# Quantized-weight stage of a vision tower: ScalarE converts one half of the codes ahead, one more mask slot on each side, and buffers placed elsewhere

## The chip, the core and the metric

The kernel runs on one NeuronCore of a Trainium2 chip. Times are microseconds of device time, the median of several executions. The engines are PE (TensorE), DVE (VectorE), ACT (ScalarE), POOL (GpSimd) and SP (SyncE, which here only issues DMA transfers). Each works through its own instructions in order and waits on semaphores.

## What is computed

The input is 32 sequences of 64 positions with 64 complex coefficients each; a filter with 64 modes spreads it to 1024 features, and two layers follow. Cut to its steps, the reference is:

```
h = _L0_tok_ref(L0_tok_A_abslog, L0_tok_A_phase, x, 1024)      # sum over 64 modes of exp(dtA * t)
h = h + _L0_attn_ref(_layernorm(h, axis=-1), Wq, Wk, Wv, Wo)   # 16 heads, rotary, causal
h = h + _L0_ffn_ref(_layernorm(h, axis=-1), w_idx, absmax, bias)
h = h + _L1_attn_ref(_layernorm(h, axis=-1), ...)              # selective state space scan
h = h + _L1_ffn_ref(_layernorm(h, axis=-1), ...)               # base + top-2 of 8 low-rank experts
```

The part that matters here is the first step and the weights of the third:

```
# the filter: K[h, l] = sum_n Cc[h, n] * exp(dtA[h, n] * l), h = 2 * K.real
# the weights: 1024 x 1024 codes of 0 to 15
w = NF4_CODE[w_idx.reshape(-1, BLOCK)] * absmax[:, None]
return jnp.einsum('bsi,oi->bso', x, w) + bias
```

## The kernel before

Everything is float32 in SBUF. The 2048 tokens are worked on in four blocks of 512 (`NBLK`), and most of the kernel is, per block, a row of weight strips of 128 x 1024 that ACT and POOL split in two parts each and PE multiplies. That begins behind an **opening stage**, the only part in which the change moves instructions. It does two things side by side.

*Weights.* The codes are turned into weights in 16 **halves** (`HALVES`; half i is one half of strip i // 2). For a half, SP loads the codes into `dqi` (two slots, i % 2), ACT converts them to bf16 in `dqf` (two slots; L573). The 16 codes stand in 8 pairs. For 5 pairs DVE writes a mask by comparing with the code (`mkd`, L1272), for 3 pairs ACT does with Abs and Relu (`away`, then `mka`, L579 and L583). PE multiplies each mask with diagonals of the code's value and adds up in `psx` (L853): per half 30 matmuls on DVE's masks, then 14 on ACT's. DVE then multiplies by the block maxima (`weights`, L1283, run behind the masks of the next half) and SP stores the result. Mask slots are rings: `RING_ACT` = 2 and `RING_DVE` = 3; a mask waits until PE has used the one that was in its slot (`s_useda`, `s_usedd`).

*The filter.* DVE and ACT build tables of Sin and Exp (DVE L1288 to L1374, ACT L594 to L606); DVE makes the factors `high` and `low` of eight positions (`powers(g)`, L1388 to L1395), PE multiplies them (`filters(g)`, L875, 32 matmuls), and ACT copies the result to the filtered sequence `hT` (`copies(g)`, L589). There are 8 groups g.

*The order* is written out by hand. Halves 0 to 4 (`EARLY`) stand ahead of the groups. Behind the filters of group g stand the halves of `LATE[g]`, on PE, DVE and ACT alike:

```
LATE = [[5, 6], [7], [8, 9], [10], [11, 12], [13], [14], [15]]
```

On ACT the copies of group g stand behind the masks of these halves, and `filters(g + 1)` needs room in `psg` that the copies make. SP's loop over the halves decides when codes are loaded:

```
for i in range(HALVES):
    m, q = i // 2, i % 2
    if i + 2 < HALVES:
        sp.wait_ge(s_dqf, i + 1)
        load_codes(i + 2)
    sp.wait_ge(s_dq, i + 1)
    sp.dma_start(w_ffn[m, :, q * HALF:(q + 1) * HALF], dqw[:, q, :]).then_inc(s_dqw[q], 16)
```

`s_dq` counts the halves whose weights DVE has written, `s_dqf` the converted ones. Behind the last half SP stores three blocks of `hT` to memory (L454), and DVE waits for two of these stores (`v.wait_ge(s_keep, 32)`) before it writes the first `xc` (L1415).

Buffers are placed by hand: each `with ExitStack()` block starts again at the address where the block before it started, so what is in different blocks lies over one another. `hT` lies over `u` and the 16 slots of [P, T] behind it.

Of the kernel before, what the change touches and what calls it, by code (L numbers as in the profile page):

```python
# [14 lines left out]
F32 = mybir.dt.float32  # L15
F32R = mybir.dt.float32r
# [6 lines left out]
P = 128  # L23
NSEQ, S, E = 32, 64, 1024
NMODE = 64
KC = E // P
NB = 8
NBLK = NSEQ // NB
T = NB * S
# [18 lines left out]
NQ = NST // 4  # L48
XT = T // P
# [82 lines left out]
PAIRS = 8  # L132
BY_ACT = 3
BY_DVE = PAIRS - BY_ACT
RING_ACT, RING_DVE = 2, 3
HALF = KC * P // 2
HALVES = 2 * KC
FG = 8
# [37 lines left out]
def tower(nc, ins, out, nblk=NBLK, stop=9):  # L176
    with ExitStack() as ctx:
# [3 lines left out]
        def sb(name, shape, dt=F32, c=ctx):  # L181
            return c.enter_context(nc.sbuf_tensor("sb_" + name, shape, dt))
# [14 lines left out]
        def C(name, a=0, n=None):  # L197
            c0, w = CCOL[name]
            return cst[:, c0 + a:c0 + (w if n is None else a + n)]
# [35 lines left out]
        u = sb("u", [P, DC, T])  # L235

        with ExitStack() as c:
            xc = sb("xc", [P, KC, T], F32, c)
            xh = sb("xh", [P, KC, T], F32R, c)
            xl = sb("xl", [P, KC, T], F32R, c)  # L240
            ah = sb("ah", [P, KC, T], F32R, c)
            al = sb("al", [P, KC, T], F32R, c)
            rstd = sb("rstd", [P, T], F32, c)
            rcos = sb("rcos", [P, NB, S], F32, c)
            rsin = sb("rsin", [P, NB, S], F32, c)
            with ExitStack() as c2:
                qc = sb("qc", [P, T], F32, c2)
                qs = sb("qs", [P, T], F32, c2)
                kc = sb("kc", [P, T], F32, c2)
                ks = sb("ks", [P, T], F32, c2)  # L250
                vf = sb("vf", [P, T], F32, c2)
                vT = sb("vT", [P, T], F32, c2)
                sm = sb("sm", [P, NB, S], F32, c2)
                pT = sb("pT", [P, T], F32, c2)
                ao = sb("ao", [P, NB, S], F32, c2)
                smx = sb("smx", [P, 2, NB], F32, c2)
            with ExitStack() as c2:
                sq = sb("sq", [P, 2, T], F32, c2)
                tA = sb("tA", [P, T], F32, c2)
                tB = sb("tB", [P, T], F32, c2)  # L260
                cv = sb("cv", [P, 2, NB, S], F32, c2)
                rt = sb("rt", [P, 8, 32], F32, c2)
        with ExitStack() as c:
            sb("over_x", [P, 3 * KC, T], F32, c)
            wT = sb("wT", [P, T], F32, c)
            w16 = sb("w16", [P, T // P, P], F32, c)
            hwh = sb("hwh", [P, T], F32R, c)
            hwl = sb("hwl", [P, T], F32R, c)
        with ExitStack() as c:
            sb("over_ah", [P, 4 * KC, T], F32, c)  # L270
            gt = sb("gt", [P, 2, T], F32, c)
            xsh = sb("xsh", [P, T], F32R, c)
            xsl = sb("xsl", [P, T], F32R, c)
            pick = sb("pick", [P, NST, P], F32R, c)
        with ExitStack() as c:
            cb_hi = sb("cb_hi", [P, 2, NB, 4, S], F32, c)
            wst = sb("wst", [P, RING, NB, 4, S], F32, c)
            twin = sb("twin", [P, 2, T], F32, c)
            gin = sb("gin", [P, 2, T], F32, c)
            dgB = sb("dgB", [P, XT, NQ, 2, 4, 32], F32, c)  # L280
            dA = sb("dA", [P, RING, NB, 4, S], F32, c)
            duT = sb("duT", [P, 2, T], F32, c)
            du = sb("du", [P, T], F32, c)
            spt = sb("spt", [P, 2, T], F32, c)
            dlt = sb("dlt", [P, 2, T], F32, c)
            wdt = sb("wdt", [RDT, 2, P], F32, c)
            dgD = sb("dgD", [P, 2, P], F32, c)
        with ExitStack() as c:
            yh = sb("yh", [P, DC, T], F32R, c)
            yl = sb("yl", [P, DC, T], F32R, c)  # L290
            lb = [sb(f"lb{n}", [P, KC, P], F32R, c) for n in range(2)]
        psg = ctx.enter_context(nc.psum_tensor("psg", [P, 4, 512], F32))
        psx = ctx.enter_context(nc.psum_tensor("psx", [P, 4, 512], F32))

# [267 lines left out]
        def _(act):  # L562
# [1 line left out]
            act.sem_inc(s_strip, CR_STRIP)  # L564
            act.wait_ge(s_mode, 80)

            def masks(i):

                q = i % 2
                act.wait_ge(s_dqi[q], i // 2 * 32 + 32)  # L570
                if i >= 2:
                    act.wait_ge(s_mkd, (i - 1) * BY_DVE)
                A(dqf[:, q, :, :], dqi[:, q, :, :], ACT.Copy).then_inc(s_dqf, 1)  # L573
                act.wait_ge(s_dqf, i + 1)
                for j in range(BY_ACT):
                    at = i * BY_ACT + j
                    if at >= 2:
                        act.wait_ge(s_mka, at - 1)
                    A(away[:, at % 2, :, :], dqf[:, q, :, :], ACT.Abs, bias=C("minus", BY_DVE + j, 1)).then_inc(s_away, 1)  # L579
                    act.wait_ge(s_away, at + 1)  # L580
                    if at >= RING_ACT:
                        act.wait_ge(s_useda, at - RING_ACT + 1)
                    A(mka[:, at % RING_ACT, :, :], away[:, at % 2, :, :], ACT.Relu, bias=C("one"), scale=-1.0).then_inc(s_mka, 1)  # L583

            def copies(g):

                for n in range(4 * g, 4 * g + 4):
                    act.wait_ge(s_filt, n + 1)
                    A(hT[:, :, :, :, 2 * n:2 * n + 2].rearrange("p b k c e -> p (b k c) e"),  # L589
                      psg[:, n % 4, :].rearrange("p (e x) -> p x e", e=2), ACT.Copy).then_inc(s_hT, 1)  # L590

            masks(0)
            act.wait_ge(s_tab, TAB_SIN[0])
            A(tab[:, 0, :, :], tab[:, 0, :, :], ACT.Sin, bias=0.0).then_inc(s_tabA, 1)  # L594
            masks(1)
            act.wait_ge(s_tab, TAB_SIN[1])
            A(tab[:, 1, :, :], tab[:, 1, :, :], ACT.Sin, bias=0.0).then_inc(s_tabA, 1)
            masks(2)
            act.wait_ge(s_tab, TAB_SIN[2])
            A(tabs[:, :, :, :], tabs[:, :, :, :], ACT.Sin, bias=0.0).then_inc(s_tabA, 1)  # L600
# [1184 lines left out]
```

## Time and profile before

| | us |
|---|---|
| median of 3 runs (4456.22 to 4457.9) | 4457.05 |
| profiled execution, its own time | 4457.86 |
| its span | 4455.4 |
| PE busy | 4153.1 (93% of the span) |
| DVE busy | 2748.4 (62%) |
| ACT busy | 2013.5 (45%) |
| POOL busy | 2180.9 (49%) |

The span runs from the first to the last instruction on the engines. A share over the whole span says little about the opening stage, which is the first 250 us of it and has limits of its own. `PEclk` is the granted clock of PE as a share of full speed: 1.00 is 2.4 GHz, 0.50 is 1.2 GHz.

### The profile page before, as it was taken

How to read it: one execution, taken by the hardware profiler on the slowest of the kernel's cores; microseconds unless marked ns; L12 is line 12 of the kernel's file. 1: busy time of each engine (PE TensorE's matmuls, PEld its weight loads, DVE VectorE, ACT ScalarE, POOL GpSimd, SP SyncE). 2: the span in 40 equal slices, each digit the busy share in tenths (PEclk: the TensorE clock that was granted, in tenths of full speed). 3: DMA queues.
4: the chain of work that ended last, by engine and by line, in shares of the span. 5: the costliest groups of instructions: out<-in, count | busy, mean ns of one | idle time of the engine just before them, and what ended most of it. 6: DMA issues, size and time to landing. Idle time of an engine off the chain costs nothing.

```text
span 4455.4 us, 58954 instructions
## 1 busy us (share of the span) xinstructions
PE 4153.1 (93%) x22688; PEld 2736.2 (61%) x22688; DVE 2748.4 (62%) x2907; ACT 2013.5 (45%) x2938; POOL 2180.9 (49%) x912
## 2 busy tenths in 40 slices
PE   3879999899999999999999999999999999989998
PEld 1557777444677777544577777644377777744467
DVE  7744463899344374599634455399934447379943
ACT  5632244777232233677422224477632223467731
POOL 0023333788523333588633333388833333378852
PEclk7989999999989999999989999999999999999998
DMA  3332223000322223200122223300022222310021
GB/s 93 84 120 72 71 100 109 29 14 16 113 71 72 76 66 121 68 14 17 62 86 84 71 76 109 100 12 17 34 95 83 74 67 81 125 42 17 14 83 62
DMA packets 93813, 303.18 MB, mean 68 GB/s; under 512 B 11648, under 2 KB 15872, under 8 KB 91008
## 3 DMA queue, kind: packets, MB, share of 16 engines
q1 hardware_dynamic: 84352, 282.98, 19.5%
q10 hardware_dynamic: 9216, 16.78, 1.0%
q8 instruction: 172, 2.82, 0.3%
q14 instruction: 73, 0.60, 0.0%
HBM read 255.68 MB, written 44.04 MB: 67 GB/s over the span
## 4 chain that ended last, share of the span: by engine, by line
PE 81%; DVE 10%; issue 6%; ACT 1%; DMA 1%; POOL 0%; DVEq 0%; POOLq 0%; ACTq 0%
PE psg L896 39%; PE psx L1074 9%; PE psg L1089 8%; DVE sb_wst L1610 6%; PE psg L923 5%; PE psx L911 3%; PE psg L932 2%; PE psx L1005 2%; PE psg L1103 1%; PE psx L1018 1%; PE psg L1051 1%; PE psx L1116 1%; PE psg L1100 1%; PE psx L1204 1%; DVE psg L1583 1%
## 5 line engine op out<-in xcount | busy, mean ns | idle before, releaser
L521 POOL TENSOR_TENSOR sb_wl<-sb_raw,sb_wh 128x1024 fp32r<-128x1024 f32 x388 | 973.6, 2512 | 2064.5 <-ACT sb_wh L619 2064.2
L1610 DVE TENSOR_TENSOR_SCAN sb_wst<-sb_dA,psx 128x1024 f32<-128x1024 f32 x512 | 1140.1, 2271 | 36.8 <-ACT sb_dA L742 23.7
L619 ACT ACTIVATE sb_wh<-sb_raw 128x1024 fp32r<-128x1024 f32 x388 | 408.3, 1053 | 624.4 <-PE psg L896 323.3
L1074 PEld LDWEIGHTS psx<-sb_dgB,sb_duT 64*128 64x128 f32 x4096 | 358.7, 189 | 526.6 <-DVE sb_wst L1610 266.4
L742 ACT ACTIVATE sb_dA<-sb_dlt,sb_a_sb 128x504 f32<-128x504 f32 x1024 | 646.4, 705 | 61.2 <-DVE sb_wst L1610 55.5
L1074 PE MATMUL psx<-sb_dgB,sb_duT 64*128 64x256 f32 x4096 | 590.8, 408 | 85.6 <-DVE sb_wst L1610 83.8
L554 POOL TENSOR_TENSOR sb_wst<-sb_wst,sb_cb_lo 128x1024 f32<-128x1024 f32 x256 | 599.2, 2362 | 90.1 <-DVE sb_wst L1610 90.1
L554 POOL TENSOR_TENSOR sb_wst<-sb_wst,sb_cb_hi 128x1024 f32<-128x1024 f32 x256 | 598.4, 2358 | 75.5 <-DVE sb_wst L1610 75.5
L1089 PE MATMUL psg<-sb_wst,sb_cst 64*64 64x512 f32 x4096 | 564.8, 624 | 10.3 <-POOL sb_wst L554 9.6
L896 PE MATMUL psg<-sb_xh,sb_wh 128*128 128x512 f32 x2112 | 558.4, 407 | 0.0
L896 PE MATMUL psg<-sb_xh,sb_wl 128*128 128x512 f32 x2112 | 522.4, 389 | 0.0
L896 PE MATMUL psg<-sb_xl,sb_wh 128*128 128x512 f32 x2112 | 521.9, 389 | 0.0
L896 PEld LDWEIGHTS psg<-sb_xh,sb_wh 128*128 128x128 f32 x2112 | 398.7, 192 | 106.3 <-issue 24.6
L896 PEld LDWEIGHTS psg<-sb_xh,sb_wl 128*128 128x128 f32 x2112 | 396.6, 188 | 84.3
L896 PEld LDWEIGHTS psg<-sb_xl,sb_wh 128*128 128x128 f32 x2112 | 396.4, 188 | 82.3
L1089 PEld LDWEIGHTS psg<-sb_wst,sb_cst 64*64 64x64 f32 x4096 | 109.2, 133 | 212.2 <-issue 212.2
L1648 DVE TENSOR_TENSOR psg<-psg,sb_rstd 128x512 f32<-128x512 f32 x64 | 44.8, 700 | 306.3 <-PE psg L896 306.3
L1680 DVE TENSOR_TENSOR sb_h<-sb_h,psg 128x512 f32 x32 | 22.0, 688 | 258.1 <-PE psg L896 137.2
L1572 DVE SCALAR_TENSOR_TENSOR sb_cv<-psg,sb_conv,sb_cv 128x504 f32<-128x504 f32 (+2 forms) x192 | 141.0, 735 | 27.8 <-DVE sb_cv L1570 4.2
L923 PE MATMUL psg<-sb_xh,sb_wh 128*128 128x512 f32 x192 | 119.4, 622 | 29.5 <-ACT sb_xh L627 29.5
L911 PE MATMUL psx<-sb_sq,sb_cst 128*128 128x512 f32 x256 | 143.1, 642 | 0.0
L733 ACT ACTIVATE sb_twin<-psg 128x512 f32<-128x512 f32 x128 | 69.5, 595 | 161.9 <-PE psg L1089 161.9
(269 smaller groups left out, 5233.6 us busy)
## 6 DMA issues: line engine op xcount, KB each, us to landing
sb_raw<-in_w SPq DMA_DIRECT2D x360, 512.0 KB, 3.5
sb_raw<-w_ffn_dequantized SPq DMA_DIRECT2D x32, 512.0 KB, 3.2
gates<-sb_gt ACTq DMA_DIRECT2D x64, 256.0 KB, 2.2
sb_gin<-gates SPq DMA_DIRECT2D x64, 256.0 KB, 2.6
sb_dqi<-in_w_idx SPq DMA_DIRECT2D x32, 256.0 KB, 4.9
h_after_tok<-sb_h SPq DMA_DIRECT2D x4, 2048.0 KB, 8.7
sb_h<-h_after_tok SPq DMA_DIRECT2D x4, 2048.0 KB, 7.8
out<-sb_h SPq DMA_DIRECT2D x4, 2048.0 KB, 7.3
```

What stands on the lines that cost most here:

```text
L521: pool.tensor_tensor(rest(b, i0), raw[:, i0 % RAW, :, :], high(b, i0).bitcast(F32), ALU.subtract).then_inc(s_wl, 1)
L554: pool.tensor_tensor(x, x, cb, ALU.mult).then_inc(s_p, 1)
L619: A(high(b, i0), raw[:, i0 % RAW, :, :], ACT.Copy).then_inc(s_wh, 1)
L742: ins_ = A(dA[:, (m * NQ + k) % RING, :, n, 1:S], dlt[:, m % 2, :].rearrange("p (b s) -> p b s", b=NB)[:, :, 1:S], ACT.Exp, scale=a_sb[:, ...
L896: ins_ = mm(psg[:, bank, :], w_[:, s_, k, :], x_[:, k0 + k, :], start=start and n == 0, stop=stop_ and n == 3 * KC - 1)
L911: mm(psx[:, 1, :], C("mean"), sq[:, k % 2, :], start=(k == 0), stop=(k == KC - 1)).then_inc(s_squ, 1)
L923: mm(psg[:, banks[s], :], w_[:, slot(b, i0 + s), k, :], X[:, kk, :], start=(k == 0 and n == 0 and not (one_chunk and s)), stop=False)
L932: ins_ = mm(psg[:, banks[s], :], wh[:, slot(b, i0 + s), k, :], Xl[:, kk, :], start=False, stop=(k == KC - 1 and not (one_chunk and not s)))
L1074: ins_ = mm(psx[:, 2 * j + r, :].rearrange("p (a t e) -> p a t e", a=8, e=2)[:, :, :, e], duT[r0:r0 + 64, m % 2, i * P:(i + 1) * P], dgB[r ...
L1089: ins_ = mm(psg[64 * c:64 * c + 64, r, :], C("fold")[r0:r0 + 64, :], wst[r0:r0 + 64, (m * NQ + k) % RING, :, 2 * half + c, :], start=(k == ...
L1572: ins_ = stt(y[:, :, d:S], x[:, :, 0:S - d], tap(3 - d), y[:, :, d:S], ALU.mult, ALU.add)
L1610: v.tensor_tensor_scan(wst[:, x, 4 * j:4 * j + 4, :, :].rearrange("p b n s -> p (b n s)"), dA[:, x, 4 * j:4 * j + 4, :, :].rearrange("p b ...
```

## The change

`RING_ACT` becomes 3 and `RING_DVE` 4. On ACT the conversion leaves `masks(i)` and becomes a function `converted(i)`; `masks(0)` calls it for halves 0 and 1, each later `masks(i)` calls `converted(i + 1)` ahead of its own masks. Its waits stay the same expressions of the half that it converts. To make room for the slots, buffers of the opening stage behind `mka` lie 2 to 4 KB higher per partition, and of the buffers that are used later `ah` and `al` now lie over the last two blocks of `hT`, `xc`, `xh` and `xl` behind them; `lb0`, `lb1`, `dgB`, `wst`, `twin`, `gin`, `gt`, `yh`, `yl` and others move with them. Every buffer that moves does so by a multiple of 2 KB.

```diff
-RING_ACT, RING_DVE = 2, 3
+RING_ACT, RING_DVE = 3, 4
...
+            ah = sb("ah", [P, KC, T], F32R, c)
+            al = sb("al", [P, KC, T], F32R, c)
             xc = sb("xc", [P, KC, T], F32, c)
             xh = sb("xh", [P, KC, T], F32R, c)
             xl = sb("xl", [P, KC, T], F32R, c)
-            ah = sb("ah", [P, KC, T], F32R, c)
-            al = sb("al", [P, KC, T], F32R, c)
...
         with ExitStack() as c:
-            sb("over_x", [P, 3 * KC, T], F32, c)
+            lb = [sb(f"lb{n}", [P, KC, P], F32R, c) for n in range(2)]
...
         with ExitStack() as c:
-            sb("over_ah", [P, 4 * KC, T], F32, c)
+            sb("over_a", [P, 2 * KC, T], F32, c)
...
             cb_hi = sb("cb_hi", [P, 2, NB, 4, S], F32, c)
+            dgB = sb("dgB", [P, XT, NQ, 2, 4, 32], F32, c)
...
-            dgB = sb("dgB", [P, XT, NQ, 2, 4, 32], F32, c)
...
         with ExitStack() as c:
+            sb("over_ah", [P, KC, T], F32, c)
             yh = sb("yh", [P, DC, T], F32R, c)
             yl = sb("yl", [P, DC, T], F32R, c)
-            lb = [sb(f"lb{n}", [P, KC, P], F32R, c) for n in range(2)]
...
-            def masks(i):
+            def converted(i):
 
                 q = i % 2
                 act.wait_ge(s_dqi[q], i // 2 * 32 + 32)
                 if i >= 2:
                     act.wait_ge(s_mkd, (i - 1) * BY_DVE)
                 A(dqf[:, q, :, :], dqi[:, q, :, :], ACT.Copy).then_inc(s_dqf, 1)
+
+            def masks(i):
+
+                q = i % 2
+                if i == 0:
+                    converted(0)
+                if i + 1 < HALVES:
+                    converted(i + 1)
                 act.wait_ge(s_dqf, i + 1)
```

On PE, DVE, POOL and SP the order of instructions is the same before and after. On ACT it moves as follows. First the start of the program, before, up to the first Sin (L594) and the conversion of half 1; the brackets name the semaphores that an instruction waits on:

```order
L573 ACTIVATE sb_dqf<-sb_dqi 128x1024 [waits s_mode]
L579 ACTIVATE sb_away<-sb_dqf,sb_cst 128x1024 [waits s_dqf]
L583 ACTIVATE sb_mka<-sb_away,sb_cst 128x1024 [waits s_away]
L579 ACTIVATE sb_away<-sb_dqf,sb_cst 128x1024
L583 ACTIVATE sb_mka<-sb_away,sb_cst 128x1024 [waits s_away]
L579 ACTIVATE sb_away<-sb_dqf,sb_cst 128x1024 [waits s_mka]
L583 ACTIVATE sb_mka<-sb_away,sb_cst 128x1024 [waits s_useda,s_away]
L594 ACT_TABLE_LOAD
L594 ACTIVATE sb_tab<-sb_tab 128x2048 [waits s_tab]
L573 ACTIVATE sb_dqf<-sb_dqi 128x1024 [waits s_dqi1]
```

and now (behind L573 the lines are 8 higher):

```order
L573 ACTIVATE sb_dqf<-sb_dqi 128x1024 [waits s_mode]
L573 ACTIVATE sb_dqf<-sb_dqi 128x1024 [waits s_dqi1]
L587 ACTIVATE sb_away<-sb_dqf,sb_cst 128x1024 [waits s_dqf]
L591 ACTIVATE sb_mka<-sb_away,sb_cst 128x1024 [waits s_away]
L587 ACTIVATE sb_away<-sb_dqf,sb_cst 128x1024
L591 ACTIVATE sb_mka<-sb_away,sb_cst 128x1024 [waits s_away]
L587 ACTIVATE sb_away<-sb_dqf,sb_cst 128x1024 [waits s_mka]
L591 ACTIVATE sb_mka<-sb_away,sb_cst 128x1024 [waits s_away]
L602 ACT_TABLE_LOAD
L602 ACTIVATE sb_tab<-sb_tab 128x2048 [waits s_tab]
L573 ACTIVATE sb_dqf<-sb_dqi 128x1024 [waits s_mkd,s_dqi0]
```

The third mask of half 0 no longer waits on `s_useda`. The conversion behind the Sin is that of half 2 instead of half 1, and it now waits on `s_mkd` too.

The second place is group 0 of the filter: half 5 and the head of half 6 on ACT. Before:

```order
L573 ACTIVATE sb_dqf<-sb_dqi 128x1024 [waits s_mkd,s_dqi1]
L579 ACTIVATE sb_away<-sb_dqf,sb_cst 128x1024 [waits s_mka,s_dqf]
L583 ACTIVATE sb_mka<-sb_away,sb_cst 128x1024 [waits s_useda,s_away]
...
L583 ACTIVATE sb_mka<-sb_away,sb_cst 128x1024 [waits s_useda,s_away]
L573 ACTIVATE sb_dqf<-sb_dqi 128x1024 [waits s_mkd,s_dqi0]
L579 ACTIVATE sb_away<-sb_dqf,sb_cst 128x1024 [waits s_mka,s_dqf]
```

and now:

```order
L573 ACTIVATE sb_dqf<-sb_dqi 128x1024 [waits s_mkd,s_dqi0]
L587 ACTIVATE sb_away<-sb_dqf,sb_cst 128x1024 [waits s_mka,s_dqf]
L591 ACTIVATE sb_mka<-sb_away,sb_cst 128x1024 [waits s_useda,s_away]
...
L591 ACTIVATE sb_mka<-sb_away,sb_cst 128x1024 [waits s_useda,s_away]
L573 ACTIVATE sb_dqf<-sb_dqi 128x1024 [waits s_mkd,s_dqi1]
L587 ACTIVATE sb_away<-sb_dqf,sb_cst 128x1024 [waits s_mka,s_dqf]
```

The rows are alike but for the slot of `dqi`: ahead of half 5's masks stands the conversion of half 6 (slot 0) instead of half 5 (slot 1), ahead of half 6's masks that of half 7.

## Rows read from the trace of the kernel before

A row of a timeline has the start and the duration in us, the engine (PEq, SPq: its queue), the line, the operation, out<-in, the number of instructions merged and, in brackets, how long the engine idled before them and what ended that. A row of windows has the stretch, its length, then busy time and number of instructions of PE, PE's weight loads, DVE, ACT and POOL, then the granted clock, the DMA share and GB/s. "DMA to landing" is the time from the start of a request to its arrival.

**Rows 1.** The page: its first line

```profile
span 4455.4 us, 58954 instructions
```

**Rows 2.** Windows of the opening stage

```profile
7.00:120.00 113.00, 39.38 (x226) 19.88 (x227) 92.77 (x132) 56.59 (x51) 0.00 (x0) 0.74 0.34 85
120.00:250.00 130.00, 114.22 (x737) 75.73 (x736) 87.54 (x140) 94.32 (x104) 0.00 (x0) 0.99 0.31 81
```

**Rows 3.** Waits from 0 to 250 us: total, times, longest

```profile
ACT sb_mka L583 <- PE psx L853: 87.2, 13, 26.2
```

**Rows 4.** Timeline of DVE, half 0

```profile
22.52 0.49 DVE L1272 TENSOR_SCALAR sb_mkd<-sb_dqf,sb_cst 128x1024 bf16<-128x1024 bf16 x1 [0.89 <-PE psx L853]
23.80 0.49 DVE L1272 TENSOR_SCALAR sb_mkd<-sb_dqf,sb_cst 128x1024 bf16<-128x1024 bf16 x1 [0.79 <-PE psx L853]
```

**Rows 5.** Timeline of DVE and ACT, up to the Exp

```profile
39.03 0.69 DVE L1283 TENSOR_TENSOR sb_dqw<-psx,sb_dqa 128x512 f32<-128x512 f32 x1
...
58.28 0.96 DVE L1328 TENSOR_TENSOR sb_etabs<-sb_mode,sb_cst 128x768 f32<-128x768 f32 x1
...
66.21 1.15 ACT L583 ACTIVATE sb_mka<-sb_away,sb_cst 128x1024 bf16<-128x1024 bf16 x1 [14.47 <-PE psx L853]
...
70.25 1.91 ACT L604 ACTIVATE sb_etab<-sb_etab 128x2048 f32<-128x2048 f32 x1
...
72.92 2.29 DVE L1335 TENSOR_TENSOR sb_tab<-sb_tab,sb_etab 128x2048 f32<-128x2048 f32 x1 [9.12 <-ACT sb_etabs L605]
```

**Rows 6.** Timeline of DVE, SP, PE and ACT, 117 to 175 us

```profile
117.36 9.59 PE L875 MATMUL psg<-sb_high,sb_low 128*128 128x256 f32 x32 [18.64 <-DVE sb_low L1395]
...
127.77 0.49 DVE L1272 TENSOR_SCALAR sb_mkd<-sb_dqf,sb_cst 128x1024 bf16<-128x1024 bf16 x1 [0.80 <-PE psx L853]
128.42 0.49 DVE L1272 TENSOR_SCALAR sb_mkd<-sb_dqf,sb_cst 128x1024 bf16<-128x1024 bf16 x1 [0.16 <-PE psx L853]
128.82 0.68 DVE L1283 TENSOR_TENSOR sb_dqw<-psx,sb_dqa 128x512 f32<-128x512 f32 x1
...
130.40 1.26 SPq L399 DMA_DIRECT2D sb_dqi<-in_w_idx  x2
...
140.60 7.14 PE L875 MATMUL psg<-sb_high,sb_low 128*128 128x256 f32 x32 [0.17 <-ACT sb_hT L589]
...
153.05 0.41 PE L853 MATMUL psx<-sb_mka,sb_dg 128*64 128x512 bf16 x2 [0.66 <-ACT sb_mka L583]
153.64 1.53 PE L875 MATMUL psg<-sb_high,sb_low 128*128 128x256 f32 x6 [0.18 <-ACT sb_hT L589]
...
165.95 1.04 ACT L573 ACTIVATE sb_dqf<-sb_dqi 128x1024 bf16<-128x1024 int32 x1
...
173.70 1.58 ACT L589 ACTIVATE sb_hT<-psg 128x512 f32<-128x512 f32 x3
...
174.44 0.89 PE L875 MATMUL psg<-sb_high,sb_low 128*128 128x256 f32 x3 [0.18 <-ACT sb_hT L589]
```

**Rows 7.** Requests into sb_dqi: landing of all requests, then at 131.0 and 185.7

```profile
DMA to landing us min/median/max: 4.0/4.9/15.7
...
DMA to landing us min/median/max: 4.8/5.1/5.4
...
DMA to landing us min/median/max: 5.2/5.7/6.1
```

**Rows 8.** Windows: PE's busy time and granted clock

```profile
117.40:122.20 4.80, 4.80 (x11) 3.83 (x12) 4.80 (x9) 0.00 (x0) 0.00 (x0) 0.50 0.00 0
245.00:248.50 3.50, 1.57 (x14) 0.48 (x10) 0.69 (x1) 2.88 (x5) 0.00 (x0) 1.00 0.18 69
248.90:251.90 3.00, 3.00 (x4) 1.45 (x5) 0.00 (x0) 1.12 (x1) 0.00 (x0) 0.50 0.52 132
```

**Rows 9.** Timeline of DVE, end of the stage

```profile
247.27 0.69 DVE L1283 TENSOR_TENSOR sb_dqw<-psx,sb_dqa 128x512 f32<-128x512 f32 x1 [3.21 <-PE psx L853]
266.20 1.88 DVE L1415 TENSOR_TENSOR sb_xc<-sb_hT,psx 128x512 f32<-128x512 f32 x3 [18.24 <-DMA h_after_tok<-sb_hT]
```

## The prediction

> **What bounds the kernel now.** The profiled execution took 4457.86 us, of which 4455.4 us are the span [rows 1]; 2.5 us lie around it. The median of the three timed runs is 4457.05 us. I sum shifts inside the span, and carry them over to the median one for one.
>
> Every instruction that the change moves, and every ring that it widens, is in the opening stage, from 0 to about 250 us: the order of SP, POOL, PE and DVE is the same in both programs. So I read that stage alone. The windows split it in two [rows 2]. Up to 120 us DVE is busy for 92.8 of 113 us and PE for 39: DVE's chain of small table operations sets the pace. From 120 to 250 us PE is busy for 114 of 130 us, ACT for 94, DVE for 88: there PE and ACT hand work to each other. The waits of the stage then say what the three wait for [rows 3]: ACT's mask writes waited 87.2 us in 13 places for PE to release a mask slot. DVE's mask writes wait for PE too [rows 4, 6]. Only what lies on the path counts of either.
>
> **First part: DVE's chain up to 120 us.** With three slots DVE can write masks 0 to 2 of a half, then waits for PE to use mask 0 before it writes mask 3, and for mask 1 before mask 4. In half 0 these two waits end at 22.52 and 23.80 [rows 4]. With four slots mask 3 needs no wait, and mask 4 takes the place that mask 3 had: it starts at 22.52. DVE is done 1.28 us sooner. PE runs at its slow clock at the start of each of the first five halves, so this repeats: 5 x 1.28 = 6.4 us.
>
> The second gain is one long wait. ACT's third mask of half 2 stood 14.47 us behind PE (slot 0 of two was still in use), the Sin of the tables and the Exp stood behind it, and DVE's product with the Exp waited 9.12 us more, until 72.92 [rows 5]. With three slots the third mask of a half needs only a slot that was used in the half before, so ACT can reach the Exp before its input exists. What is late next? ACT must now convert half 3 ahead of the masks of half 2, and SP requests the codes of half 3 only after DVE has written the weights of half 0. These ended at 39.7 [rows 5], now 2 x 1.28 us sooner, at 37.2; with a trip of 6.9 us (below) the codes are there at 44.1. The conversion and six mask operations take 7.8 us (165.95 to 173.70 in [rows 6]), Sin and table load 2.9 us (from the end of L583 at 67.4 to 70.25 in [rows 5]): ACT is ready for the Exp at 54.8. Its input comes from DVE at 59.2 - 2.6 = 56.7 [rows 5], so ACT has 1.9 us of cover. The Exps take 2.7 us (70.25 to 72.92) and end at 59.4; DVE, 3 x 1.28 us ahead of before, wants them at 72.92 - 9.12 - 3.84 = 60.0. So the whole 9.1 us goes. Together, half 5's dequantization on PE starts 6.4 + 9.1 = **15.5 us earlier**, at 111.4.
>
> **Second part: the wait that takes its place.** `masks(i)` now begins with `converted(i + 1)`. Behind that instruction, on an engine that works in order, stand the six operations of half i's masks and the four copies of the filtered sequence; PE's last three pairs of half i and the next group of filters wait for those. The conversion needs the codes of half i + 1. SP requests them only after it has stored the weights of half i - 2, which DVE writes behind its masks of half i - 1. (The conversion also waits for those masks themselves, `s_mkd`; that wait ends just ahead of the weights, so it is never the later one.) Where two halves stand behind one group of filters (groups 0, 2 and 4), this trip becomes the longest path:
> - In half 5 DVE's last two masks start at 127.77 and 128.42 [rows 6]; with one slot more the last starts at 127.77, which saves 0.65 us. The weights then end 2.6 - 0.65 = 1.95 us after PE began the half (129.50 before; PE began at 126.9, when its cold filters of 9.59 us ended).
> - From the end of the weights to the codes: SP starts its second request of 256 KB at about 131.0, 1.5 us later [rows 6], and it lands 5.4 us after that [rows 7]: 6.9 us. Another landed 6.1 us after its start, the quickest of all 4.0 us [rows 7], so the trip is 5.5 to 7.6 us. I take 6.9 for group 0, 6.7 for the others.
> - From the start of a conversion to the start of the next filters, with no wait between: 165.95 to 174.44 [rows 6], 8.5 us.
>
> Group 0, from PE's start of half 5 to the next filters: 1.95 + 6.9 + 8.5 = 17.35 us; before, 126.9 to 140.60, 13.7 us. **3.6 us longer.** Groups 2 and 4, from filters to filters: 7.1 (the filters, [rows 6]) + 1.95 + 6.7 + 8.5 = 24.25 us; before, 153.64 to 174.44, 20.8 us. **3.45 us longer, twice.**
>
> Groups 1, 3, 5, 6 and 7 have one half each, and there the codes landed long before. What is left is PE's own work. Before, PE waited 0.66 us for ACT's last mask, its last pair took 0.41, and the filters came 0.18 us later still [rows 6]; the filters at 153.64 would have started near 152.6 without it. **5 x 1.05 = 5.2 us shorter.** Half 15's conversion waits for the weights of half 12, one group earlier; in group 6 that lands some 4 us into the filters and costs 0.5 us: 3.9 + 8.5 = 12.4 us against 11.9.
>
> **Third part: PE's clock.** In the new two-half groups PE starts the second half 12.1 us behind the group's filters and has used DVE's masks at 15.4. ACT starts its conversion at 15.75 and has the first mask 3.4 us later: PE idles 3.8 us, and then 1.6 us ahead of each of the next two masks, which come 2.2 us apart and take 0.64 and 0.2 us: some 1.5 us of work in 9. The trace shows what such a stretch does. From 245.0 to 248.5 PE was busy for 1.57 of 3.5 us, and the 3 us behind it ran at a granted clock of 0.50, that is 1.2 GHz instead of 2.4 [rows 8]. PE will be emptier than that in these stretches, so I expect the filters behind each of the three groups to start at 1.2 GHz. What that costs, one group shows: the filters at 117.36 started at 0.50 [rows 8] and took 9.59 us, those at 140.60 took 7.14 [rows 6]. **3 x 2.4 = 7.2 us.** The Trainium skill (TensorE: Matmul & The Clock Gate, HAM oscillation) says the same of bursts with DMA waits between: the wait lets the array be throttled again, and the next burst starts cold, every time. By that rule the sum is the one below with the 7.2 us; if the clock stayed up, it would be 7.2 us lower. This kernel's own rows side with the rule.
>
> **Fourth part: the end of the stage and the places.** SP stores the last weights behind PE's last pair (DVE's operation at 247.27), then the filtered sequence; DVE waits 18.24 us for those stores until 266.20 [rows 9]. `v.wait_ge(s_keep, 32)` still stands there, though `xc` no longer lies over the filtered sequence, so this wait stays whole and the stage after shifts as a block. The other buffers keep their sizes and their instructions; no row of before shows a duration that depends on a buffer's place, so I put that at 0, within 2 us either way.
>
> **Sum.** -15.5 + 3.6 + 2 x 3.45 - 5.2 + 0.5 = -9.7; with the clock, -9.7 + 7.2 = **-2.5 us**. That gives 4455.4 us for the profiled execution, and 4454.6 us for the median.
>
> **Rivals.**
> - *The clock stays up.* Then -9.7: 4447.4 us. For it: from 120 to 250 us the granted clock was 0.99 in the mean, waits and all [rows 2]. Against it: the fall in [rows 8] came with more work than these gaps hold.
> - *Slower: DVE's wait for the Exp comes back.* If the codes of half 3 land later than the 1.9 us of cover allows, DVE waits again. From about 4.4 us late on, the kernel is slower than before; if the whole 9.1 us return, -2.5 + 9.1 = +6.6: 4463.7 us. Longer trips push the same way: 0.7 us more at each of the three groups (7.4 to 7.6 us, the upper end of [rows 7]) is +2 us. For it: one load of codes took 15.7 us, against a median of 4.9 [rows 7]; it was requested near the start, among the loads of the whole input. It is half 2's, and lands near 30, in time for half 1's masks to end near 38. Against it: the codes of half 3 are requested at 38 us, when those loads are done.
> - *The trip is hidden.* If something else holds the second conversion off the path, the pairs would run at ACT's pace. Two halves are then 2 x 7.8 us and four copies 2 us, 17.6 us against 20.8, which saves 3.2 us in each of the three groups. With no fall of the clock that is -15.5 - 9.6 - 5.2 = -30 us: 4427 us. Nothing in the order of SP speaks for it, since the request stands behind the weights.
>
> **How the numbers follow.** A measurement of this kernel tells about 0.2% (8.9 us) from no change, so the bounds are 4448.1 and 4466. Forecast (three slow starts, long trips), 4450 to 4459: 0.62. Clock stays up, at least in part, 4443 to 4450: 0.20. Exp wait or longer trips, 4459 to 4466: 0.11. Trip hidden, below 4440: 0.05. Anything slower still: 0.02. The range takes in the first two and half of the third: 4444 to 4461. Faster by over 0.2%: most of the second and all of the fourth, 0.2. Slower by over 0.2%: 0.04. The same: 0.76.
>
> **What would show it** (lines numbered as before; behind L573 the changed file is 8 lines longer). Right: DVE L1335's wait is gone and the L875 filters start near 102 us; ACT's L573 waits for the DMA of `sb_dqi` at three to five places with 3 us or more each; ACT no longer waits at its last mask; the second, fourth and sixth group of filters (about 129, 167 and 206 us) take some 9.5 us with a granted clock near 0.5 at their start; DVE's last L1283 starts near 245 us; from there on each instruction has the distance that it had. Wrong: filters of 7.1 us behind the pairs (then the clock term goes), pairs of 21 us or less (the trip is off the path), or a stage after 250 us that is longer or shorter by itself (places matter).

## The result and the profile after

| | before | after |
|---|---|---|
| median, us | 4457.45 (20 runs, 4455.94 to 4459.47) | 4450.41 (20 runs, 4445.77 to 4452.36) |
| profiled execution, us | 4457.86 | 4449.22 |
| its span, us | 4455.4 | 4447.1 |

The ratio of after to before is 0.9983, with a 95% interval of 0.9976 to 0.999: 7.0 us less. The time lies inside the predicted range, 4.2 us below the predicted 4454.6. The gain itself, 7.0 us, is nearly three times the 2.5 us that were forecast. It is within 0.2% of before, though the interval leaves out 1. The head of the page after, beside [rows 1]:

```profile
span 4447.1 us, 58953 instructions
## 1 busy us (share of the span) xinstructions
PE 4153.7 (93%) x22688; PEld 2736.7 (62%) x22688; DVE 2746.8 (62%) x2907; ACT 2013.7 (45%) x2938; POOL 2180.6 (49%) x912
```

No engine has other work; only waits changed. The windows of the opening stage, beside [rows 2]:

```profile
7.00:120.00 113.00, 52.20 (x326) 28.73 (x326) 105.32 (x154) 59.06 (x54) 0.00 (x0) 0.79 0.39 97
120.00:250.00 130.00, 111.40 (x650) 70.81 (x650) 73.59 (x118) 92.72 (x103) 1.04 (x1) 0.92 0.29 82
```

Up to 120 us DVE is busy for 105.3 us where it was 92.8: it waits 12.5 us less in this stretch. From 120 to 250 us the mean granted clock fell from 0.99 to 0.92. The waits from 0 to 250 us, beside [rows 3]:

```profile
ACT sb_dqf L573 <- DMA sb_dqi<-in_w_idx: 74.7, 12, 26.1
...
DVE sb_mkd L1280 <- PE psx L861: 48.9, 19, 9.5
...
PE psx L861 <- ACT sb_mka L591: 20.1, 13, 3.7
...
ACT sb_etab L612 <- DVE sb_etabs L1336: 1.7, 1, 1.7
```

ACT's 87.2 us of waits for PE at its mask write are gone. In their place stand 74.7 us at the conversion, for codes. Some of that is harmless, like the wait for PE before it; what counts is whether PE then waits for ACT. The timeline of DVE and ACT in the first part, beside [rows 4] and [rows 5]:

```profile
22.40 0.49 DVE L1280 TENSOR_SCALAR sb_mkd<-sb_dqf,sb_cst 128x1024 bf16<-128x1024 bf16 x1 [0.49 <-PE psx L861]
...
59.77 2.28 DVE L1343 TENSOR_TENSOR sb_tab<-sb_tab,sb_etab 128x2048 f32<-128x2048 f32 x1
...
43.81 1.06 ACT L573 ACTIVATE sb_dqf<-sb_dqi 128x1024 bf16<-128x1024 int32 x1 [2.51 <-DMA sb_dqi<-in_w_idx]
...
56.61 1.91 ACT L612 ACTIVATE sb_etab<-sb_etab 128x2048 f32<-128x2048 f32 x1 [1.71 <-DVE sb_etabs L1336]
```

In the first five halves DVE now has at most one wait per half instead of two, and its product with the Exp (L1343) starts at 59.77 without a wait. ACT had the codes of half 3 at 43.81 and still waited 1.71 us for the Exp's input. The timeline of PE, DVE, SP and ACT over the first groups, beside [rows 6]:

```profile
111.22 3.43 PE L861 MATMUL psx<-sb_mkd,sb_dg 128*64 128x512 bf16 x30
...
112.50 0.68 DVE L1291 TENSOR_TENSOR sb_dqw<-psx,sb_dqa 128x512 f32<-128x512 f32 x1
...
114.08 1.26 SPq L399 DMA_DIRECT2D sb_dqi<-in_w_idx  x2
...
119.74 1.06 ACT L573 ACTIVATE sb_dqf<-sb_dqi 128x1024 bf16<-128x1024 int32 x1 [26.07 <-DMA sb_dqi<-in_w_idx]
...
115.99 3.40 PE L861 MATMUL psx<-sb_mkd,sb_dg 128*64 128x512 bf16 x30
123.07 0.84 PE L861 MATMUL psx<-sb_mka,sb_dg 128*64 128x512 bf16 x6 [3.67 <-ACT sb_mka L591]
125.29 1.49 PE L861 MATMUL psx<-sb_mka,sb_dg 128*64 128x512 bf16 x6 [1.38 <-ACT sb_mka L591]
127.51 0.64 PE L861 MATMUL psx<-sb_mka,sb_dg 128*64 128x512 bf16 x2 [0.73 <-ACT sb_mka L591]
128.11 8.56 PE L883 MATMUL psg<-sb_high,sb_low 128*128 128x256 f32 x32
...
141.47 7.17 PE L883 MATMUL psg<-sb_high,sb_low 128*128 128x256 f32 x32
...
165.13 8.83 PE L883 MATMUL psg<-sb_high,sb_low 128*128 128x256 f32 x32
...
178.75 7.17 PE L883 MATMUL psg<-sb_high,sb_low 128*128 128x256 f32 x32
```

This is the whole mechanism in one place. DVE writes weights (of half 4) at 112.50; SP requests codes (of half 7) behind them at 114.08; ACT gets them at 119.74; PE, which had finished DVE's masks of half 6 at 119.4 (115.99 + 3.40), waits 3.67, 1.38 and 0.73 us for ACT's masks; and the filters behind the pair take 8.56 us instead of 7.17. The windows show the clock there, beside [rows 8]:

```profile
119.60:123.00 3.40, 0.00 (x0) 0.00 (x0) 3.40 (x7) 3.23 (x4) 0.00 (x0) 1.00 0.81 195
124.40:127.90 3.50, 1.88 (x8) 0.49 (x8) 3.47 (x6) 3.47 (x5) 0.00 (x0) 0.50 0.01 2
128.20:130.90 2.70, 2.70 (x7) 2.17 (x8) 0.00 (x0) 2.70 (x5) 0.00 (x0) 0.50 0.02 6
131.20:136.40 5.20, 5.20 (x26) 4.48 (x24) 0.00 (x0) 5.10 (x6) 0.00 (x0) 1.00 0.00 0
```

The granted clock was at 2.4 GHz while PE idled, fell to 1.2 GHz behind the idle stretch, and was back at 2.4 GHz some 3 us into the filters. The end of the stage on DVE and SP, beside [rows 9]:

```profile
240.95 0.69 DVE L1291 TENSOR_TENSOR sb_dqw<-psx,sb_dqa 128x512 f32<-128x512 f32 x1 [3.02 <-PE psx L861]
260.01 1.88 DVE L1423 TENSOR_TENSOR sb_xc<-sb_hT,psx 128x512 f32<-128x512 f32 x3 [18.37 <-DMA h_after_tok<-sb_hT]
...
243.78 0.81 SPq L446 DMA_DIRECT2D sb_raw<-in_w  x2
```

The last weights come 6.3 us sooner (247.27 before), and DVE's wait for the stores stays: 18.37 us against 18.24.

### The profile page after: what moved, and what is told of

The parts are those of the page before. It is cut to its first block, busy times and chain, and to the rows that moved or that the text cites. A ratio compares the mean times of both kernels' runs of the same rounds, so it can differ in the third digit from the quotient of the medians.

```text
span 4447.1 us, 58953 instructions
## 1 busy us (share of the span) xinstructions
PE 4153.7 (93%) x22688; PEld 2736.7 (62%) x22688; DVE 2746.8 (62%) x2907; ACT 2013.7 (45%) x2938; POOL 2180.6 (49%) x912
## 4 chain that ended last, share of the span: by engine, by line
PE 81%; DVE 10%; issue 6%; ACT 1%; DMA 1%; POOL 0%; DVEq 0%; POOLq 0%; ACTq 0%
PE psg L904 39%; PE psx L1082 9%; PE psg L1097 8%; DVE sb_wst L1618 6%; PE psg L931 5%; PE psx L919 3%; PE psg L940 2%; PE psx L1013 2%; PE psg L1111 1%; PE psx L1026 1%; PE psg L1059 1%; PE psx L1124 1%; PE psg L1108 1%; PE psx L1212 1%; DVE psg L1591 1%
## 5 line engine op out<-in xcount | busy, mean ns | idle before, releaser
L1618 DVE TENSOR_TENSOR_SCAN sb_wst<-sb_dA,psx 128x1024 f32<-128x1024 f32 x512 | 1140.4, 2271 | 37.3 <-ACT sb_dA L750 23.7
```

Source lines behind the costliest of these rows:

```text
L1618: v.tensor_tensor_scan(wst[:, x, 4 * j:4 * j + 4, :, :].rearrange("p b n s -> p (b n s)"), dA[:, x, 4 * j:4 * j + 4, :, :].rearrange("p b ...
```

## The experiments

The theory is the prediction's: the longer rings take waits off the path, and converting ahead puts a trip of the codes and a cold PE on it. The rival readings are that the conversion ahead is what removes the waits, that the moved buffers matter, and that the trip is a matter of DMA speed and not of where the request stands. Each kernel starts from after; "old order" is this edit:

```diff
             def masks(i):
-                if i == 0:
-                    converted(0)
-                if i + 1 < HALVES:
-                    converted(i + 1)
+                converted(i)
```

**The long rings alone** (old order, `RING_ACT, RING_DVE = 3, 4`).

> The longer rings and the new places stay, the conversion goes back: half i is converted at the head of its own masks. If my account holds, the gain of 15.5 us ahead of half 5 stays, the trip for the codes leaves the path, and the groups of two halves run at ACT's pace: about 17.4 us from filters to filters instead of 23.7 to 24.1, group 0 about 10.2 instead of 16.9, and the filters behind them start at full clock. Sum -15.5 - 3.5 - 6.8 - 5.2 = -31: about 4426 us, 24 us faster than the changed kernel. Rival: the conversion ahead is itself worth something, since DVE no longer waits for it (16.7 us of such waits before); then this kernel is slower than the changed one, above 4450 us.

Measured: 4425.87 us, ratio 0.993 (0.9914 to 0.9945) to before: 32 us less than before and 24.5 less than after. Timeline of PE and DVE:

```profile
101.04 10.02 PE L880 MATMUL psg<-sb_high,sb_low 128*128 128x256 f32 x32 [18.40 <-DVE sb_low L1400]
...
121.39 7.14 PE L880 MATMUL psg<-sb_high,sb_low 128*128 128x256 f32 x32 [0.18 <-ACT sb_hT L594]
...
133.34 7.17 PE L880 MATMUL psg<-sb_high,sb_low 128*128 128x256 f32 x32
...
150.86 7.14 PE L880 MATMUL psg<-sb_high,sb_low 128*128 128x256 f32 x32 [0.19 <-ACT sb_hT L594]
...
235.69 1.88 DVE L1420 TENSOR_TENSOR sb_xc<-sb_hT,psx 128x512 f32<-128x512 f32 x3 [18.67 <-DMA h_after_tok<-sb_hT]
```

The first group starts at 101.04, as in after (101.24), so the whole gain of the first part belongs to the rings. A pair of halves takes 17.5 us (133.34 to 150.86) against 20.8 before and 23.7 after, and no filters behind a pair are cold.

**The conversion ahead alone** (`RING_ACT, RING_DVE = 2, 3`).

> The conversion ahead and the new places stay, the rings go back to two and three slots. If the conversion ahead only costs, nothing is gained ahead of half 5, the groups of two halves are 3.3 us longer each and the filters behind them start cold (1.5 us each): about 4457 + 14 = 4471 us, slower than before by 0.3%. Rival (the conversion ahead brings part of the gain): below 4457 us.

Measured: 4474.73 us, ratio 1.0039 (1.0023 to 1.0054), 17 us more than before. Timeline of PE:

```profile
116.98 8.60 PE L883 MATMUL psg<-sb_high,sb_low 128*128 128x256 f32 x32 [17.95 <-DVE sb_low L1403]
...
158.36 7.14 PE L883 MATMUL psg<-sb_high,sb_low 128*128 128x256 f32 x32 [0.19 <-ACT sb_hT L597]
...
182.65 9.86 PE L883 MATMUL psg<-sb_high,sb_low 128*128 128x256 f32 x32
```

The first group starts where it did before (117.36), so converting ahead gives nothing in the first part. A pair takes 24.3 us (158.36 to 182.65), with cold filters behind it. The forecast of 4471 us was 3.7 us low: it took 1.5 us for each cold group, and the three cost 1.8, 2.7 and 1.7 us. Converting ahead costs 17 us with the short rings and 24.5 with the long ones. Most of the difference is the pair that it is added to, 20.8 us with the short rings and 17.5 with the long ones.

**The places alone** (old order, rings of 2 and 3).

> Only the buffers are at their new places; rings and order are those of before. Mine: within 1 us of before, 4456 to 4459 us. Rival: the 2 us that the stretch behind the opening stage gained in the changed kernel come from the places; then 4455 us or less, with that stretch 2 us shorter.

Measured: 4458.35 us, ratio 1.0 (0.9991 to 1.001). No effect of the places shows; the interval leaves room for some 4 us either way.

**One ring at a time** (old order).

```diff
-RING_ACT, RING_DVE = 3, 4
+RING_ACT, RING_DVE = 3, 3        # ACT's ring alone;  DVE's ring alone: 2, 4
```

> Only ScalarE's ring is longer (3 slots; DVE's has 3), the conversion stands where it was before, the places are new. By my terms DVE's wait for the Exp goes (9.1 us), the 6.4 us of DVE's own ring do not, and the groups are as short as with both rings (15.5 us less than before): about 4457.5 - 24.6 = 4433 us. Rival: the groups need DVE's ring as well; then 4440 us or more.

> Only VectorE's ring is longer (4 slots; ScalarE's has 2), the conversion stands where it was before, the places are new. By my terms DVE gains 1.28 us in each of four of the first five halves, while the gain of half 2 is lost in the wait for the Exp, and the groups stay as before since ScalarE's third mask still waits for PE: about 4457.5 - 5.1 = 4452 us. Rival: the rings gain together and this one gains nothing alone: 4457 us.

Measured: 4432.24 us with ACT's ring, ratio 0.9942 (0.9927 to 0.9957), and 4452.74 with DVE's, ratio 0.9986 (0.9977 to 0.9995). Against the 4458.35 of the places alone that is 26.1 and 5.6 us, together 31.7; the two at once gave 32.5. Within the noise the two are additive. The first group of filters starts at 106.92 with ACT's ring and at 112.21 with DVE's (116.93 with neither): 10.0 and 4.7 us of the first part. Added to ACT's ring, DVE's is worth 5.9 us there (106.92 to 101.04). The pairs come from ACT's ring: 17.5 us with it, 20.8 without.

**The request for codes ahead of the weights of the half before.** The conversion stays ahead; SP requests the codes of half i + 2 before it waits for and stores the weights of half i - 1.

```diff
-            for i in range(HALVES):
-                m, q = i // 2, i % 2
+            for i in range(HALVES + 1):
                 if i + 2 < HALVES:
                     sp.wait_ge(s_dqf, i + 1)
                     load_codes(i + 2)
-                sp.wait_ge(s_dq, i + 1)
-                sp.dma_start(w_ffn[m, :, q * HALF:(q + 1) * HALF], dqw[:, q, :]).then_inc(s_dqw[q], 16)
-                if i + 2 < HALVES:
-                    load_absmax(i + 2)
+                if i >= 1:
+                    m, q = (i - 1) // 2, (i - 1) % 2
+                    sp.wait_ge(s_dq, i)
+                    sp.dma_start(w_ffn[m, :, q * HALF:(q + 1) * HALF], dqw[:, q, :]).then_inc(s_dqw[q], 16)
+                    if i + 1 < HALVES:
+                        load_absmax(i + 1)
```

> The changed kernel, but SP requests the codes of half i + 3 behind the weights of half i - 1 instead of half i: the store of each half's weights moves behind the next request. The order on ACT, PE and DVE is that of the changed kernel. If it is the late request that makes the groups of two halves long, they shrink to about 17.5 us and the clock stays up: about 4426 us, as with the rings alone. Rival: it is the conversion's other wait, for all of DVE's masks of the half before; then the groups stay at 23 us or more and the time stays above 4445 us.

Measured: 4423.17 us, ratio 0.9922 (0.9906 to 0.9937). Waits and timeline of PE:

```profile
ACT sb_dqf L574 <- DVE sb_mkd L1281: 28.2, 4, 23.8
...
ACT sb_dqf L574 <- DMA sb_dqi<-in_w_idx: 6.3, 2, 5.4
```

```profile
120.20 7.14 PE L884 MATMUL psg<-sb_high,sb_low 128*128 128x256 f32 x32 [0.18 <-ACT sb_hT L598]
132.15 7.17 PE L884 MATMUL psg<-sb_high,sb_low 128*128 128x256 f32 x32
...
149.66 7.14 PE L884 MATMUL psg<-sb_high,sb_low 128*128 128x256 f32 x32 [0.18 <-ACT sb_hT L598]
```

With the same transfers at the same sizes, requested one step earlier in SP's order, the conversion's wait for codes falls from 74.7 us in 12 places to 6.3 in two, and the pairs are back at 17.5 us. So it was the place of the request and not the speed of the transfer. What remains, 28.2 us for DVE's masks, does not lengthen the pairs: they take what they take with the rings alone. Against the rings alone, the conversion ahead then brings 2.7 us by the medians; the two intervals overlap, so I don't call that a gain.

**PE kept busy in the gaps.** In halves 6, 9 and 12 matmuls of `dg` with itself into an unused bank stand ahead of each of ACT's masks; their results are never read.

```diff
                 for j in range(BY_ACT):
                     at = i * BY_ACT + j
+                    if i in (6, 9, 12):
+                        for n in range(15 if j == 0 else 6):
+                            for r in range(2):
+                                mm(psx[64 * r:64 * r + 64, 2, :], dg[:, 0, :].bitcast(BF16), ...)
                     pe.wait_ge(s_mka, at + 1)
```

> The changed kernel with extra matmuls of constants into an unused bank of psx, issued where PE waits for ScalarE's masks in the second half of each group of two (halves 6, 9, 12): about 3.2, 1.3 and 1.3 us of work in gaps of 3.3, 1.4 and 0.7 us. If the slow start of the filters behind these groups is PE's clock alone, they take 7.2 us instead of 8.5 to 8.8, and the groups keep their length to 0.6 us: 3 to 5 us less than the changed kernel, 4446 to 4448 us. Rival: the filters are slow for another reason; then they stay at 8.5 us and the time is 4450 us or more.

Measured: 4444.63 us, ratio 0.997 (0.9958 to 0.9982). Timeline of PE:

```profile
118.31 3.40 PE L874 MATMUL psx<-sb_dg 128*64 128x512 bf16 x30
...
127.37 7.14 PE L888 MATMUL psg<-sb_high,sb_low 128*128 128x256 f32 x32 [0.18 <-ACT sb_hT L597]
139.31 7.17 PE L888 MATMUL psg<-sb_high,sb_low 128*128 128x256 f32 x32
...
162.90 7.14 PE L888 MATMUL psg<-sb_high,sb_low 128*128 128x256 f32 x32 [0.20 <-ACT sb_hT L597]
```

The pairs are as long as in after (139.31 to 162.90 is 23.6 us), but the filters behind them take 7.14 us instead of 8.56 to 8.83. The granted clock is 1.00 from 118.3 to 134.5. That separates the two costs: the trip stays, the cold start goes. By medians it is 5.8 us less than after. Of this 0.9 us was there before the first added matmul (half 5's last pairs end at 115.2 against 116.2), and the three filters account for 4.7 (26.1 us together in after, 21.4 here).

**The best version: the long rings, old order, and the stores off the path.** The wait for two stores of the filtered sequence moves from DVE's first norm to the first writes of `ah` and `al`, which now lie over it, and SP requests strips 2 and 3 behind the first of the three stores instead of behind all.

```diff
                         for n in (2, 3, 1):
                             sp.dma_start(h0[n], ...)
-                        first_strips(0, 2, 4)
+                            if n == 2:
+                                first_strips(0, 2, 4)
...
-                        v.wait_ge(s_keep, 32)
...
+                            if b == 0 and j == 1:
+                                v.wait_ge(s_keep, 32)      # and the same on ACT ahead of ah
```

> The longer rings without the conversion ahead, and one use of the new places: xc no longer lies over the filtered sequence, so DVE's wait for its stores moves to the first writes of ah and al, and SP requests weight strips 2 and 3 behind the first of the three stores instead of behind all of them. If the stores' 6 MB in front of these strips are what holds the first norm, the strip lands some 10 us sooner and the time is about 4416 us. Rival: strips and stores share the DMA engines and the stage keeps its length: 4425 us.

Measured: 4416.93 us, ratio 0.9907 (0.9892 to 0.9922): 41 us less than before, 33 less than after, and 8.9 less than the rings alone. Timeline of DVE and SP:

```profile
223.95 1.88 DVE L1423 TENSOR_TENSOR sb_xc<-sb_hT,psx 128x512 f32<-128x512 f32 x3 [7.25 <-PE psx L951]
...
226.74 2.62 SPq L446 DMA_DIRECT2D sb_raw<-in_w  x2
229.41 0.91 SPq L454 DMA_DIRECT2D h_after_tok<-sb_hT  x2
```

The norm starts 11.7 us sooner (235.69 with the rings alone) and waits for PE now. ACT's conversion of the third strip starts at 231.56 instead of 241.74; the time at the end is 8.9 us less. The two edits weren't tried apart. The new places are what makes this allowed, since `xc` no longer lies over the filtered sequence; the change as made moved the buffers and left the wait.

## Why the prediction was right, and where it was off

**The first part: right.** Half 5 was to start at 111.4 on PE, 15.5 us sooner; it starts at 111.22, 15.7 sooner. The Exp wait went whole, as said, with 1.71 us of cover left at the Exp where 1.9 was predicted. The single rings confirm the split. ACT's ring alone gave 10.0 us where its term was 9.1. The term of DVE's ring, 6.4 us, holds beside the longer ACT ring, and there it gave 5.9; alone it gave 4.7, where 5.1 was expected, since the gain of half 2 is lost in the wait for the Exp. One reason given for the 6.4 is not seen in half 0: the granted clock was 0.50 at the start of halves 1 to 3 and 0.58 in half 4, but the profile has 1.00 in half 0 (20.8 to 23.8), though DVE's two waits end 1.28 us apart there as well.

**The trip: right, a little long.** From the end of the weights to the conversion it took 6.56 us in group 0 (113.18 to 119.74; 6.9 taken), and 6.22 and 6.68 us in groups 2 and 4 (6.7 taken). From the conversion to the filters it took 8.37 us (8.5 taken). Group 0 then took 16.9 us (17.35 predicted), groups 2 and 4 took 23.66 and 24.11 us (24.25 predicted), and group 6 took 12.50 (12.4 predicted). The experiment on SP's request showed that this wait comes from the place of the request. ACT's conversion waited 3 us or more for codes in eight places, where three to five were forecast; only the pairs and, by 0.5 us, group 6 grew longer by it.

**The cold filters: right in kind, the mis-sized term.** The prediction took 3 x 2.4 = 7.2 us, by a group whose filters took 9.59 us. The filters behind the pairs took 8.56, 8.83 and 8.73 us against 7.17: 1.39, 1.66 and 1.56, 4.6 us in all. The group at 117.36 ran cold for all of its first 4.8 us [rows 8]; here the cold part began earlier, at the few matmuls on ACT's masks, when PE waited for ACT anyway, and only the last 3 us of it fell on the filters. The 7.2 us were 2.6 too many, and that is 2.6 of the 4.2 us by which the forecast was high. By the Trainium skill (TensorE: Matmul & The Clock Gate, HAM oscillation) a wait between bursts makes the next burst start cold each time. The trace agrees in all three groups, and PE kept busy took the cold starts away; but here the first burst behind the wait was the cheap one on ACT's masks, and it took up part of the cold stretch.

The 2.4 us was also only one draw: the first group of filters stands directly behind 17 to 19 us of idling in all ten kernels, and took from 8.60 us (the conversion ahead alone) to 10.05 (after). The cold part of a group's filters cost 1.4 to 2.9 us there, and no row of before tells which it will be.

**The sum.** Up to the last weights the prediction had -2.5 us, and -6.3 was measured (247.27 to 240.95). Of the 3.8 us between, 2.6 are the clock, 0.2 the first part, and 1.2 the three pairs (0.45 + 0.6 + 0.15, by the lengths above), 4.0 together; 0.1 the other way is in group 6, and 0.1 is left over.

**Behind the stage: not quite zero, and not the places.** The profiled spans differ by 8.3 us, 2.0 more than the last weights do. Two windows of before, from SP's first strip request to the end of the span and over the cold part of the first norm:

```profile
250.10:4455.40 4205.30, 3999.41 (x21727) 2640.50 (x21726) 2568.03 (x2636) 1862.57 (x2783) 2180.73 (x908) 0.97 0.20 67
273.50:279.40 5.90, 5.20 (x9) 2.87 (x10) 5.31 (x6) 3.79 (x8) 2.37 (x1) 0.51 0.29 92
```

and the same of after:

```profile
243.78:4447.10 4203.32, 3995.13 (x21724) 2639.04 (x21722) 2567.70 (x2636) 1863.02 (x2783) 2180.39 (x908) 0.97 0.20 67
267.20:270.80 3.60, 2.93 (x5) 1.73 (x6) 3.04 (x3) 2.61 (x6) 2.37 (x1) 0.50 0.02 5
```

The rest of the kernel is 2.0 us shorter. In the first norm PE's clock was low for some 5.9 us before and 3.6 us after. Measured the same way, the seven experiments that have after's places and leave the end of the stage as it is give 4203.63 (ACT's ring alone), 4203.72 (PE kept busy), 4203.74 (the rings alone), 4204.35 (conversion ahead alone), 4204.85 (places alone), 4205.33 (DVE's ring alone, 244.97 to 4450.3) and 4205.44 (codes requested sooner). So these 2 us come and go with the same places; they aren't due to where the buffers lie. That the timing of the clock's changes decides them fits the two windows, but only one of several such changes was looked at, and no run isolates it: this stays open.

**The rivals.** "The clock stays up" gave 4447.4 us, which is closer to the measured time (3.0 us) than the forecast is (4.2 us). So the time alone does not speak for the forecast; the traces do, since the clock fell in all three groups. "The Exp wait comes back" did not happen. "The trip is hidden" did not happen either, and the rings alone and the sooner request show what it would have been: 4427 us by the prediction's arithmetic, 4425.87 and 4423.17 measured.

**Where the gain went.** The rings are worth 32 us. Of that the conversion ahead costs 24.5. By the traces of after and of the rings alone, three pairs are longer by 6.5, 6.1 and 6.6 us (16.9 against 10.4, 23.66 and 24.11 against 17.52), three cold filters cost 4.6, and group 6 0.5: 24.3 us together.

## What to carry to other kernels

A longer ring and an earlier conversion look like one idea but are two. Try them apart: the rings took away the waits, and the step ahead only moved the need for its input forward, past the place in another engine's queue where that input is requested. Before an operation is moved ahead, find where its input is requested and what stands in front of that request in its queue; move the request with it. And where a buffer's move makes an old wait needless, look at moving the wait too: here that, with two requests ahead of the stores, was worth another 8.9 us.

## What the runs showed that was not expected

- A cold start has no fixed price. Filters of 32 matmuls took 7.14 to 7.17 us at 2.4 GHz, 8.56 to 8.98 us behind gaps with a few matmuls of masks between (once 9.86), and 8.60 to 10.05 us directly behind 17 to 19 us of idling. In after the clock was 0.50 over the filters' first 5.7 us (101.3 to 107.0), in the kernel with the sooner request over some 3 us (100.9 to 103.8), behind idle stretches of 17.8 and 18.1 us.
- In the third pair of the kernel with the conversion ahead alone PE waited only 2.64, 1.38 and 0.73 us for ACT's masks, with matmuls between, and the filters behind were cold all the same (8.87 us). The mean granted clock of [rows 2], 0.99 with waits in every pair, was no guide to what somewhat longer ones would do.
- Matmuls of no use in the gaps were worth 4.7 us over three pairs and left the pairs as long as they were (23.6 and 24.2 us): they repair the clock and not the wait.
